# List products moved into slot zero, a copy moved from GpSimd to ScalarE, and the last parts in another order

## What is computed

```
attention:  q, k: 8 heads of 128;  v: 8 heads of 64;  alpha = sigmoid((xn Wg + bg) / 16)
            state = alpha * state + k v^T;  out_t = q_t . state      (over 2048 positions)
            y1 = (out * sigmoid(xn Wog)) Wo
experts:    scores = sigmoid(xn gate_w^T);  8 of 64 experts per token, out of 4 of 8 groups
            weight = score / sum of the 8 scores * 2.5
            each expert takes its first 256 tokens in token order
            y2 = sum of weight * (silu(t w_gate) * (t w_up)) w_down
output:     x + y1 + y2
```

## Time and profile before

| | us |
|---|---|
| median of 3 runs | 1264.27 |
| the three runs | 1264.02 to 1266.55 |
| the profiled execution | 1266.82 |
| its span, first to last instruction | 1265.1 |
| granted TensorE clock in it | 1.000 |

### The profile page before, as it was taken

One profiled execution on the slowest core, in us unless ns is written; L12 is line 12 of the kernel. 1 busy time (PEld: TensorE's weight loads), 2 busy tenths in 40 slices (PEclk: granted clock), 3 DMA queues, 4 the chain that ended last, 5 costly groups with the idle time before them and its releaser, 6 DMA issues.

```text
span 1265.1 us, 28662 instructions
## 1 busy us (share of the span) xinstructions
PE 1237.9 (98%) x9910; PEld 1092.2 (86%) x9910; DVE 976.6 (77%) x2343; ACT 624.3 (49%) x1319; POOL 487.4 (39%) x377
## 2 busy tenths in 40 slices
PE   7899999999999999999999999999999999999999
PEld 6788888887888888799899998989989999889987
DVE  6997878889797659878688687786885877868844
ACT  6675756666574544344444444444444444434432
POOL 2110111011001027237467385474574754845620
PEclk9999999999999999999999999999999999999999
DMA  6576534354352322357486575674774765748665
GB/s 241 170 250 200 188 110 156 122 190 158 121 171 60 111 75 84 95 145 186 105 198 165 130 178 136 150 181 106 188 171 121 172 155 137 193 104 191 162 194 183
DMA packets 124920, 194.68 MB, mean 154 GB/s; under 512 B 12016, under 2 KB 98608, under 8 KB 124592
## 3 DMA queue, kind: packets, MB, share of 16 engines
q1 hardware_dynamic: 94384, 147.99, 36.1%
q0 software_dynamic: 30464, 45.83, 19.7%
HBM read 148.62 MB, written 57.74 MB: 163 GB/s over the span
## 4 chain that ended last, share of the span: by engine, by line
PE 76%; DVE 16%; issue 5%; ACT 2%; another core or an unknown queue 0%; DVEq 0%; DMA 0%; ACTq 0%
PE bank L793 21%; PE bank L808 7%; PE bank L905 7%; PE bank L937 7%; PE bank L845 6%; PE bank L825 5%; PE bank L877 3%; PE bank L863 3%; PE bank L866 3%; PE bank L948 3%; PE bank L836 3%; DVE Dt L1506 3%; PE bank L889 2%; PE bank L927 2%; DVE At L1527 2%
## 5 line engine op out<-in xcount | busy, mean ns | idle before, releaser
L635 POOL DMA_INDIRECT acc<-arena,idx_all x128 | 224.3, 1752 | 149.4 <-DMA acc<-res 54.1
L627 POOL DMA_INDIRECT arena<-table,idx_all x132 | 163.6, 1240 | 153.8 <-ACT share L1160 96.5
L793 PE MATMUL bank<-xp,wq 128*128 128x512 f32 x768 | 208.4, 406 | 0.0
L793 PE MATMUL bank<-xp,wk 128*128 128x512 f32 x768 | 202.2, 398 | 0.0
L793 PEld LDWEIGHTS bank<-xp,wk 128*128 128x128 f32 x768 | 138.5, 188 | 29.3 <-DVE wk L1416 0.4
L793 PEld LDWEIGHTS bank<-xp,wq 128*128 128x128 f32 x768 | 136.6, 189 | 25.4 <-issue 0.8
L1506 DVE TENSOR_TENSOR_SCAN Dt<-decay,eye_b 128x512 f32<-128x512 f32 x128 | 157.7, 1233 | 0.0
L845 PE MATMUL bank<-qT,kT 128*128 128x128 f32 x1024 | 136.2, 275 | 1.8 <-DVE At L1527 1.4
L1136 ACT ACTIVATE kT<-bank 128x512 f32<-128x512 f32 x128 | 76.7, 599 | 118.0 <-PE bank L793 102.2
L845 PEld LDWEIGHTS bank<-qT,kT 128*128 128x128 f32 x1024 | 125.2, 192 | 3.3 <-DVE At L1527 1.6
L1136 ACT ACTIVATE qT<-bank 128x512 f32<-128x512 f32 x128 | 76.9, 601 | 85.4 <-PE bank L793 64.7
(11 more groups left out here) (174 smaller groups left out, 2317.1 us busy)
## 6 DMA issues: line engine op xcount, KB each, us to landing
decay<-decay_dram SPq DMA_DIRECT2D x64, 512.0 KB
carry<-decay_dram SPq DMA_DIRECT2D x60, 512.0 KB
arena<-in_L_attn_x_dram SPq DMA_DIRECT2D x16, 512.0 KB, 4.5
table<-arena SPq DMA_DIRECT2D x16, 512.0 KB, 3.2
xT_dram<-arena SPq DMA_DIRECT2D x16, 512.0 KB, 3.0
arena<-in_L_ffn_w_gate_dram SPq DMA_DIRECT2D x64, 128.0 KB
arena<-in_L_ffn_w_up_dram SPq DMA_DIRECT2D x64, 128.0 KB
arena<-in_L_ffn_w_down_dram SPq DMA_DIRECT2D x64, 128.0 KB
```

What stands on the lines that cost most here:

```text
L627: pool.indirect_dma_start(out=xg[:, e % 2, j, :], out_offset=None, in_=table[:, :], in_offset=bass.IndirectOffsetOnAxis(ap=idx_all[:, e, j ...
L635: pool.indirect_dma_start(out=acc[:, :], out_offset=bass.IndirectOffsetOnAxis(ap=idx_all[:, e, j:j + 1], axis=0), in_=yb[:, e % 2, j, :], ...
L793: last = mm(to[:, :], w[:, part, k, h * DK:(h + 1) * DK], xp[:, other, k, :], start=(k + i == 0), stop=(k == KD - 1 and i == 2))
```

## The change

Three edits. First, the list products of the slots step begin in slot 0: four of the 16 are there, at places 2 to 5, one in slot 1, two in each of slots 2 to 6 and the last one in slot 7; before, they ran from slot 1 to slot 8. DVE's `count_four` calls stand between the projections of slot 0 and the first slot accordingly. Second, the copy of `chosen` leaves POOL; ACT takes it (`chosen_kept`), after place 3 of slots 1, 4 and 7 in a norm step and of slot 1 in the count step, with a wait for `weight_ready`. Third, at the very end pair 2 of batches 0 and 1 is no longer taken ahead of the wait for pair 3, but after it, together with pair 3.

```diff
-FOUR_AT = [(s, place) for s in range(1, H) for place in ((0, 4, 2) if s == 4 else (0, 2))] + [(H, 0)]
-FOUR_AT.sort(key=lambda at: (at[0], (0, 1, 2, 4, 3).index(at[1])))
+FOUR_AT = [(0, place) for place in range(2, 6)] + [(1, 2)]
+FOUR_AT += [(s, place) for s in range(2, H - 1) for place in (0, 2)] + [(H - 1, 0)]
...
             def weights_out(c):
                 pool.wait_ge(weight_ready, c + 1)
                 pool.dma_start(tab_tiles[c][:, :, D:XW], weight).then_inc(wt_stored, 16)
-                pool.tensor_copy(sel_all[:, :, :, c].rearrange("p e b -> p b e"), chosen).then_inc(sel_kept, 1)
...
                 proj_qk(c, kind, 0, 1)
                 if not first:
                     out_proj(c, 0)
+                beside(c, kind, 0, 2)
                 proj_v(c, kind, 2)
                 if not first:
                     out_proj(c, 1)
+                beside(c, kind, 0, 3)
                 if not is_last(c):
                     keys_back(c, 0)
                 scores(c, 0)
...
+                beside(c, kind, 0, 4)
                 proj_v(c, kind, 3)
                 if not first:
                     out_proj(c, 2)
+                beside(c, kind, 0, 5)
...
             out_part(2, (0, 1, 2))
             out_part(3, (0, 1, 2))
-            out_part(0, (2,))
-            out_part(1, (2,))
             for b in range(B):
-                out_part(b, (KO - 1,))
+                out_part(b, (2, KO - 1) if b < 2 else (KO - 1,))
...
+            def chosen_kept(c):
+                act.wait_ge(weight_ready, c + 1)
+                act.copy(sel_all[:, :, :, c].rearrange("p e b -> p b e"), chosen).then_inc(sel_kept, 1)
...
                     beside(c, kind, s, 3)
+                    if kind == "norm" and s % 3 == 1:
+                        chosen_kept(STEP_N * c + s // 3)
+                    if kind == "count" and s == 1:
+                        chosen_kept(C - 1)
                     if s % 2 == 0:
                         outs_high(c, s // 2 - 1)
...
-                if kind == "slots" and s == 0 and place == 3:
+                if kind == "slots" and s == 0 and place == 1:
                     keep_firsts()
...
                 if not is_first(c) and not is_last(c):
                     projected(c, 0, kind)
+                    beside(c, kind, 0, 2)
                     projected(c, 1, kind)
-                beside(c, kind, 0, 4)
+                beside(c, kind, 0, 3 if kind == "slots" else 4)
...
+                    if s == 1 and kind == "slots":
+                        beside(c, kind, 0, 4)
                     if s == 1 and not is_first(c) and not is_last(c):
                         projected(c, 2, kind)
+                        if kind == "slots":
+                            beside(c, kind, 0, 5)
```

More of the change, by code:

```diff
@@ L1689, in step @@
                 beside(c, kind, 0, 1)
-                if kind != "experts":
+                if kind in ("norm", "count"):
                     beside(c, kind, 0, 3)
```

## The result

The changed kernel is slower, by 12.0 us by the ratio and by 13.0 us between the medians:

| | before | changed |
|---|---|---|
| median of 4 runs | 1264.14 us | 1277.11 us |
| lowest and highest | 1263.42 to 1266.55 | 1274.81 to 1277.96 |
| ratio (95% interval) | | 1.0095 (1.0078 to 1.0113) |
| profiled execution | 1266.82 us | 1274.81 us |
| span in it | 1265.1 us | 1273.2 us |

The account below looks back on a forecast made before the run. The prediction took PE's time, plus the few places where PE stands still, as the bound. Its terms, -1.9 + 3.0 + 0.2 = +1.3 us on the median of 1264.27, gave 1265.6 us, range 1262.3 to 1268.6.

Parts of the forecast that it names:

- the length of the copy on ACT: Copy of `chosen` in ACT's queue: taken as 0.40 us, with bounds 0.37 and 1.36 us.
- the slow copy: Rival: ACT's copy, writing 32 bytes apart, is as slow as POOL's 1.36 us; 1273.8 us in all, chance 0.12.
- The queue behind the wait in slot 7: Norm steps c = 1 to 4: copy delays `kw`, so `update` and `outputs` come later, +0.44 us per step.
- Slot 4: Norm steps c = 1 to 4: copy ahead of `outs_high` delays DVE's `outs_low` through slot 8, +0.29 us per step.
- the copies are hidden: Rival: PE's wait for `At` absorbs the later `kw`, DVE loses nothing in slot 4; 1262.6 us, chance 0.18.
- c = 0: First norm step, where PE had no wait for `At`: half a step's loss from the copy, +0.35 us.
- POOL's copies: Slot 8 scans run faster without POOL's copy, 1.22 us against 1.60; gain of 0.3 us in all.
- my own forecast's case: Whole change with the copy at 0.40 us: +1.3 us, 1265.6 us on the median, chance 0.60.
- The second edit as a whole: Copy moved to ACT in the norm steps: 2.9 + 0.35 - 0.3 = +3.0 us, bounds 0 and +11.
- The first edit: Slots step: earlier list products remove PE's wait for `At` in slot 8, -1.9 us, bounds -1.3 and -2.1.
- The rival of the moved stall: Slots step: PE waits as long in slot 0 instead, first edit brings nothing; 1267.5 us, chance 0.10.
- The third edit: Kernel's end: PE reaches the wait for `g_low` just too early within the 36 products, +0.2 us, bounds 0 and +0.4.

Follow-up runs that it names:

- e7_pe_filled: Changed kernel plus 20 idle transposes ahead of `update` in slot 8 of the five norm steps; 1270.71 us beside 1263.22 for the kernel before, ratio 1.0054.
- e4_contiguous: Changed kernel with the choices table laid out by chunk, so ACT's copy writes neighbouring elements; 1263.64 us beside 1260.71 for the kernel before, ratio 1.0020.
- e2_copy_only: Kernel before with the second edit alone, the copy on ACT after place 3 of slots 1, 4, 7; 1276.20 us beside 1260.71, ratio 1.0121.
- e5_slot7_only: Changed kernel with ACT copying only in slot 7 of norm steps, other copies on POOL; 1274.72 us beside 1263.22 for the kernel before, ratio 1.0075.
- e1_lists_end: Kernel before with the first and third edit alone, the copy staying on POOL; 1258.76 us beside 1260.71, ratio 0.9984.
- e3_copy_late: Changed kernel with ACT's copies moved to the very end of slots 2, 5 and 8; 1256.52 us beside 1260.71 for the kernel before, ratio 0.9969.
- e6_slot4_only: Changed kernel with ACT copying only in slot 4 of norm steps, other copies on POOL; 1265.90 us beside 1263.22 for the kernel before, ratio 1.0017.
- e8_late_old_end: e3_copy_late with the last parts in the order of before; 1258.62 us beside 1263.22 for the kernel before, ratio 0.9962.

## Why the prediction was wrong

**The failed step is one term: the length of the copy on ACT.** "I take 0.40 us, close to the first, as it is the same engine and size" chose the nearest row by engine and size. The row that was nearest in the thing that mattered was POOL's 1.36 us: the same source, the same destination, the same stride. It measured 1.34 to 1.39 us on ACT. With neighbouring elements it measured 0.40 us, so the difference is the stride of the writes. The Trainium skill (SBUF — State Buffer, its note on SBUF cachelines in "Door 1: The DMA port swizzle") states that accesses that each go to a new 16-byte line pay a penalty. By that rule, the runs now agree: 1.36 us against 0.40 us for the same 256 elements; they hold only these two distances, 32 and 2 bytes, so where the penalty begins isn't shown. Against the slow copy I had argued with ACT rows that were all contiguous and so couldn't speak on it. The rival deserved far more than 0.12.

**The mechanism around it was right.** The queue behind the wait in slot 7 cost what the sum says once the length is right: 3.28 us from the weights to `outputs` against 1.99, +1.3 us (forecast +0.44 at 0.40 us, and 2.55 against 1.99 where the copy did take 0.40). With 1.34 us put in, my sum gives 1.38. That it fits so well is in part luck, as three of its small terms were off and cancel: the copy starts 0.12 us after the weights and not 0.04, `kw` takes 1.34 us and not 1.14, and it overlaps the copy by 0.50 us and not 0.11. Slot 4 cost 2.27 - 1.09 = 1.18 us (forecast 0.29 at 0.40 us), and it reached the step's length, 0.8 to 1.2 us, as forecast. The sum of both is 2.5 us, and `outputs` of slot 8 is 2.1 to 2.5 us late in c = 1 to 4 of the filled kernel. Up to 0.5 us come back after that, probably as POOL no longer copies there, which leaves the 2.1 to 2.3 us of its steps. The rival "the copies are hidden" held in slot 1 and in the count step only. Two small terms were too small: c = 0, given half a step of 0.35 us, lost 1.3 to 2.1 us, and POOL's copies, given 0.3 us in all, had cost 2.0 us, half of it in c = 0.

**A term was missing: TensorE's clock.** I wrote that the clock enters no term, as it was 1.00 in the rows. But the change moved PE's standing time: 1.06 to 1.2 us between `update` and `outputs` became 2.6 us ahead of `update`, and the clock then fell in three of four steps, at 1.6 us each. It did not need the long copy: at 0.40 us, with 1.94 us of standing, it fell in two of four. e4_contiguous, the nearest there is to my own forecast's case, lost 2.5 us by the ratio (1.3 to 3.8), 2.9 between the medians, where I had +1.3. 0.3 us of that is its count step (68.83 us against 68.5), which its slower selections bring. The two falls in its profile are worth 3.2 us at 1.6 each, an estimate; without them its steps c = 1 to 4 would be 0.3 to 0.7 us longer, 2.0 in all where I had 2.6. So even with the right length of the copy the sum would have missed the clock. The rival with the slow copy gave 1273.8 us; three falls at 1.6 us make it 1278.7, which is 1.6 above the median of 1277.11.

The second edit as a whole, given +3.0 us, costs 14.7 us in the profile (12.8 up to the end of the slots step, and the 1.9 that the first edit gained). By rounded figures these are 1.3 in c = 0, 8.6 for the queue in c = 1 to 4, and 4.9 for the clock.

**The first edit was right**: -1.9 us forecast, 70.66 to 68.76 us measured, and -2.0 us in time for the first and third edit together. The next wait was the one named, ACT's `kw` in slot 8 (0.59 us). In slot 0 PE never stood for a comparison; all its loads that waited for POOL in the whole step come to 0.5 us. The rival of the moved stall is refuted.

**The third edit** was given +0.2 and shows +0.14 us in the profile. Its effect on the time is not measured.

**The chances** were made around one length of the copy, with a range that ended at 0.7 us although the bound from POOL's row was 1.36. The price of the far bound, 1273.8, was worked out and then left outside the range. That was the mistake in the range, apart from the clock.

## What to carry to other kernels

When an instruction moves to another engine, cost it by the row with the same access pattern before the one with the same engine: here the stride of the writes made it 3.4 times as long on ACT, and as long as it had been on POOL. A copy of 1.36 us was worth about -2 or +15 us by its place in the queue alone: put it where its input is long ready and the engine would be idle, and look at what is queued behind its wait. And where a change lengthens the stands of TensorE, give its clock a term, although it is 1.00 in every row of before: here it fell behind such stands, and no longer fell when they were filled.

## What the runs showed of the hardware that I had not expected

- ACT copied 256 elements per partition from f32 to bf16 in 0.40 us when they were written next to each other, and in 1.36 us when they were 32 bytes apart. POOL took 1.36 us for the latter as well, and 2.2 us in two of its 16 copies, both in c = 0. Reading across instead made ACT's copy of 512 bf16 elements 1.10 us long, against 0.62.
- In the profiled executions TensorE's granted clock fell to its lower level around stands of 1.9 to 2.7 us ahead of `update` in 12 of the 16 norm steps c = 1 to 4 of the changed kernel, e2_copy_only, e4_contiguous and e5_slot7_only, and in none of the 24 of the kernel before, e1_lists_end, e3_copy_late, e6_slot4_only, e7_pe_filled and e8_late_old_end, where PE stood for at most 1.3 us at a time near the end of slot 8. Between the changed kernel and e7_pe_filled, which differ in 20 transposes in that stand alone, the low level cost 1.6 us in each step in which it fell. The length of the stand alone doesn't decide it: 1.94 us brought a fall in c = 1 of e4_contiguous and none in its c = 3, and 1.71 us at the end of c = 0 brought one in e2_copy_only and none in the changed kernel.
